# Attention scores from two float32r parts instead of three bf16 parts, with the heads of a unit split over the two halves of the array's rows

## What is computed

```python
# x: (4, 512, 256); ctx: (4, 1024, 256); 16 heads of 16
q = split_heads(layernorm(x) @ Wq.T + bq)
k = split_heads(ctx @ Wk.T + bk)
v = split_heads(ctx @ Wv.T + bv)
score = einsum('bhqd,bhkd->bhqk', q, k) / sqrt(16)
out = einsum('bhqk,bhkd->bhqd', softmax(score), v)
x = x + tanh(g_xattn) * (merge_heads(out) @ Wo.T + bo)
# then layernorm, a gate that picks 2 of 8 experts, a shared expert, all in float32
```

## Time and profile before

| | |
|---|---|
| median of 3 runs | 741.25 us (738.51 to 744.33) |
| the profiled run | 741.77 us, its span 740.0 us |
| PE busy | 647.2 us (87%) |
| DVE busy | 501.3 us (68%) |
| ACT busy | 426.1 us (58%) |
| POOL busy | 242.4 us (33%) |
| granted PE clock, mean | 0.943 of 2.4 GHz |
| chain that ended last | PE 66%, issue 14%, DVE 7%, POOL 5%, DMA 3% |

### The profile page before, as it was taken

The page is one execution under the profiler, slowest core; times in us unless marked ns, Lnnn a source line. Parts: engine busy times, 40 slices in busy tenths (PEclk is TensorE's granted clock), DMA queues, the critical chain, the costliest instruction groups (busy, mean ns, idle before and its releaser), DMA issues.

```text
span 740.0 us, 12662 instructions
## 1 busy us (share of the span) xinstructions
PE 647.2 (87%) x3616; PEld 338.5 (46%) x3616; DVE 501.3 (68%) x829; ACT 426.1 (58%) x842; POOL 242.4 (33%) x240
## 2 busy tenths in 40 slices
PE   3788677879999999999999999978886969999990
PEld 3677451223233323333333332344364758888880
DVE  5799889748888888888888888547536734433430
ACT  3665244647777777777777777745523214544440
POOL 8342224033422443134000122100175503545542
PEclk9899897979999999999999999999987989999995
DMA  8879687925696687977566340010029994665545
GB/s 276 285 223 317 194 211 169 162 47 102 108 218 181 185 175 142 202 194 166 77 100 85 60 85 1 20 39 0 9 107 356 418 277 95 96 97 94 85 46 138
DMA packets 82858, 108.11 MB, mean 146 GB/s; under 512 B 16528, under 2 KB 64570, under 8 KB 81853
## 3 DMA queue, kind: packets, MB, share of 16 engines
q1 hardware_dynamic: 72080, 78.88, 45.7%
q0 software_dynamic: 10736, 28.71, 15.0%
HBM read 62.10 MB, written 47.35 MB: 148 GB/s over the span
## 4 chain that ended last, share of the span: by engine, by line
PE 66%; issue 14%; DVE 7%; POOL 5%; DMA 3%; another core or an unknown queue 2%; SPq 1%; POOLq 1%; ACT 0%; DVEq 0%; ACTq 0%
PE psO L1464 16%; PE psS L1437 16%; PE psM L1419 13%; PE psH L1682 7%; POOL parts L581 3%; PE psY L1708 3%; PE psX L1532 2%; PE psH L1638 1%; PE psH L1679 1%; PE psX L1670 1%; PE psH L1693 1%; DMA acc<-ysb,ids 1%; PE psO L1507 1%; PE psM L1437 1%
## 5 line engine op out<-in xcount | busy, mean ns | idle before, releaser
L810 ACT ACTIVATE pr<-psS 128x512 f32<-128x512 f32 x488 | 266.6, 595 | 109.2 <-PE psS L1437 109.0
L1073 DVE TENSOR_REDUCE mneg<-psM 128x1 f32<-128x1024 f32 x240 | 282.6, 1220 | 68.6 <-PE psM L1419 68.5
L1437 PE MATMUL psS<-qst,kst 99*128 99x512 bf16 x488 | 153.8, 388 | 12.1 <-DMA qst<-msb 11.5
L1464 PE MATMUL psO<-pr,vt 128*32 128x512 f32 x1024 | 138.3, 612 | 0.0
L1419 PE MATMUL psM<-kst,qst 96*128 96x512 bf16 x480 | 127.4, 386 | 6.4 <-DVE mneg L1073 4.1
L1437 PEld LDWEIGHTS psS<-qst,kst 99*128 99x128 bf16 x488 | 39.9, 97 | 160.5 <-ACT pr L810 129.9
L720 POOL DMA_INDIRECT acc<-ysb,ids x39 | 60.2, 1543 | 74.7 <-ACT ysb L933 43.9
L1419 PEld LDWEIGHTS psM<-kst,qst 96*128 96x128 bf16 x480 | 46.3, 98 | 65.5 <-DVE mneg L1073 10.6
L567 POOL TENSOR_TENSOR msb<-mcp,none 16x128 bf16<-16x128 f32 x16 | 6.2, 389 | 209.1 <-ACT mcp L787 209.0
L1682 PE MATMUL psH<-wall,zgT 128*128 x234 | 70.3, 437 | 0.0
L1308 DVE TENSOR_TENSOR rg<-psH,rs 128x256 f32<-128x256 f32 x39 | 16.6, 424 | 68.5 <-ACT rs L921 65.1
(11 more groups left out here) (244 smaller groups left out, 869.0 us busy)
## 6 DMA issues: line engine op xcount, KB each, us to landing
kst<-k_parts SPq DMA_DIRECT2D x96, 128.0 KB, 5.8
w_parts<-wraw POOLq DMA_DIRECT2D x14, 768.0 KB, 4.7
wall<-w_parts SPq DMA_DIRECT2D x7, 1536.0 KB
v_pad<-vst SPq DMA_DIRECT2D x16, 512.0 KB, 7.6
vt<-v_pad SPq DMA_DIRECT2D x16, 512.0 KB, 7.6
wraw<-wexp POOLq DMA_DIRECT2D x9, 768.0 KB, 6.7
k_parts<-parts SPq DMA_DIRECT2D x16, 384.0 KB, 6.1
qst<-q_parts SPq DMA_DIRECT2D x96, 64.0 KB, 5.3
```

The costliest lines, as they stand in the source:

```text
L810: nc.scalar.activation(pr[:, slot, j], score_bank(s, j), ACT.Exp, scale=SCALE).then_inc(e_done, 1)
L1073: V.tensor_reduce(mneg[:, parity, i:i + 1], psM[:, i % 2], X_AXIS, ALU.max, negate=True).then_inc(m_free, 1)
L1437: mm(score_bank(s, j), kst[:, slot, j, kt * P:(kt + 1) * P], qst[:, slot, j], start=True, stop=True).then_inc(s_full, 1)
L1464: last = mm(psO[j * VW:(j + 1) * VW, u % 2], vt[:, u, k, j * VW:(j + 1) * VW], pr[:, k % 4, j], start=(k == 0), stop=(k == KT - 1), skip_g ...
```

## The change

Q and K are kept as two parts of type float32r (about float32, fewer bits in each product) for three of bf16; three products of parts are summed for six. With 16 rows each these are 48 rows, with the two parts of the maximum 50. So two heads fit above each other: heads 0 and 1 of a unit have rows 0 to 49, heads 2 and 3 rows 64 to 113 (`rows_of`), and a matmul uses one half of the array's rows.

- ACT makes part 0 in one pass; DVE makes part 1 in one operation straight from `psF`, and now it is this one that frees `psF`. `kf`, `third_parts` and `k_ok` go.
- The ones in `kst` come from a small strip in SBUF by two DMAs, not from a POOL memset of the whole rows.
- POOL splits a maximum in two operations; SP sends it in four DMAs, two for each half.
- The maximum tiles are taken in another order (`max_of`): even ones from heads 2 and 3, odd ones from 0 and 1. In a step the two halves of a maximum tile stand behind one score each, and the score is in the other half of the rows.

```diff
-TERMS = ((0, 0), (0, 1), (1, 0), (1, 1), (0, 2), (2, 0))
+TERMS = ((0, 0), (0, 1), (1, 0))
 SROWS = len(TERMS) * DH
-MROWS = SROWS + 3
+PARTS = 2
+MROWS = SROWS + PARTS
+HALF = 64
+HH = 2
...
-    q_parts = dram("q_parts", [NB, 3, D, NQ], BF16)
-    k_parts = dram("k_parts", [NB, 3, D, NK], BF16)
+    q_parts = dram("q_parts", [NB, PARTS, D, NQ], F32)
+    k_parts = dram("k_parts", [NB, PARTS, D, NK], F32)
...
-        kst = sb("kst", [MROWS, NG, HG, NK], BF16, sB)
-        qst = sb("qst", [MROWS, NG, HG, NQ], BF16, sB)
+        kst = sb("kst", [HALF + MROWS, NG, HH, NK], F32R, sB)
+        qst = sb("qst", [HALF + MROWS, NG, HH, NQ], F32R, sB)
...
+        def max_of(i):
+
+            h = HH * (1 - i % 2) + i // 2 // QT
+            return h, i // 2 % QT, h * QT + i // 2 % QT
+
+        def rows_of(h, n):
+            return slice(HALF * (h // HH), HALF * (h // HH) + n)
...
+            def load_max(n, u):
+
+                for s, ready in enumerate((m_chain, mt_split)):
+                    sp.wait_ge(ready, n + 1)
+                    for half in range(2):
+                        row = HALF * half + SROWS + s
+                        sp.dma_start(qst[row:row + 1, u].bitcast(F32),
+                                     msb[half * HH * QT:(half + 1) * HH * QT, u % 2, s, :].bitcast(F32)).then_inc(m_ld[u], 16)
...
-            nc.gpsimd.memset(kst[SROWS:MROWS], 1.0).then_inc(ones_k, 1)
-            pool.wait_ge(ones_k, 1)
+            nc.gpsimd.memset(strip[:], 1.0).then_inc(strip_ok, 1)
...
                 nc.gpsimd.tensor_tensor(msb[:, parity, 0], mcp[:], none[:].to_broadcast([HG * QT, P]), ALU.subtract).then_inc(m_chain, 1)
-                pool.wait_ge(m_chain, 3 * n + 1)
-                nc.gpsimd.tensor_tensor(mcp[:], mcp[:], msb[:, parity, 0], ALU.subtract).then_inc(m_chain, 1)
...
+                pool.wait_ge(m_chain, n + 1)
+                nc.gpsimd.tensor_tensor(msb[:, parity, 1], mcp[:], msb[:, parity, 0].bitcast(F32), ALU.subtract
                                         ).then_inc(mt_split, 1)
...
-                    act.wait_ge(k_ok, i + 1)
-
                     act.wait_ge(qk_st[c], 32 * (b + 1))
-                    bias = bq_s[:, 0 if c == 2 else 1, m:m + 1]
-                    nc.scalar.activation(kf[:, m], psF[:, m], ACT.Identity, bias=bias)
                     nc.scalar.activation(parts[:, c, m, 0], psF[:, m], ACT.Identity,
-                                         bias=bias).then_inc(f_taken, 1)
+                                         bias=bias_of(c, m)).then_inc(f_hi, 1)
...
-                    dve.wait_ge(f_taken, 2 + 6 * b + 2 * c + m + 1)
-                    chain(V.tensor_tensor(kf[:, m], kf[:, m], parts[:, c, m, 0], ALU.subtract), base + m + 1)
-                    V.tensor_copy(parts[:, c, m, 1], kf[:, m]).then_inc(r_ok, 1)
+                    dve.wait_ge(f_hi, 6 * b + 2 * c + m + 1)
+                    V.scalar_tensor_tensor(out=parts[:, c, m, 1], in0=psF[:, m], scalar=bias_of(c, m),
+                                           in1=parts[:, c, m, 0].bitcast(F32), op0=ALU.add, op1=ALU.subtract).then_inc(f_taken, 1)
...
+                rows = rows_of(j, MROWS)
+                mm(score_bank(s, j), kst[rows, slot, j % HH, kt * P:(kt + 1) * P], qst[rows, slot, j % HH], start=True,
                    stop=True).then_inc(s_full, 1)
...
                     score(0)
+                    maximum(0, 0)
                     score(1)
+                    maximum(0, 1)
                     values(b, u, k)
                     score(2)
+                    maximum(1, 0)
                     score(3)
-                    for j, off, i in tiles:
...
+                    maximum(1, 1)
```

More of the change, by code:

```diff
@@ L129, in build @@
                    ("tL", [P, 3, DT, BLK], F32R)]
-        parts, vst, kf, wA_raw, ctxt, zA, wAH, wAL, tH, tL = (sb(*a, sa) for a in a_names)
+        parts, vst, wA_raw, ctxt, zA, wAH, wAL, tH, tL = (sb(*a, sa) for a in a_names)
         sa.close()
@@ L409, in first_unit @@
                 load_unit(0, 0)
+            sp.wait_ge(strip_ok, 1)
+            for half in range(2):
+                row = HALF * half + SROWS
+                sp.dma_start(kst[row:row + PARTS].rearrange("s u h t -> s u (h t)").bitcast(F32),
+                             strip[:].unsqueeze(1).to_broadcast([PARTS, NG, HH * NK])).then_inc(ones_k, 16)
             stores(0, True)
@@ L1358, in early @@
                         pe.wait_ge(m_free, 2 + i)
[L1359 removed]
+                    h, qt, _ = max_of(i)
+                    rows = rows_of(h, SROWS)
                     for half in range(2):
                         last = mm(psE[:, half * BLK:(half + 1) * BLK],
[L1362 to L1363 removed]
+                                  qst[rows, 0, h % HH, qt * P:(qt + 1) * P],
+                                  kst[rows, 0, h % HH, half * BLK:(half + 1) * BLK], start=True, stop=True)
                     last.then_inc(m_full, 1)
@@ L1410, in _, with max_half @@
             phase_a(NB - 1, True)
-            def max_tile(t, slot, i):
-                h, qt = divmod(i, QT)
-                pe.wait_ge(m_free, t + 1)
-                for half in range(2):
-                    last = mm(psM[:, i % 2, half * BLK:(half + 1) * BLK],
-                              qst[0:SROWS, slot, h, qt * P:(qt + 1) * P],
-                              kst[0:SROWS, slot, h, half * BLK:(half + 1) * BLK], start=True, stop=True)
-                last.then_inc(m_full, 1)
+            def max_half(t, slot, i, half):
+                h, qt, _ = max_of(i)
+                rows = rows_of(h, SROWS)
+                if half == 0:
+                    pe.wait_ge(m_free, t + 1)
+                last = mm(psM[:, i % 2, half * BLK:(half + 1) * BLK],
+                          qst[rows, slot, h % HH, qt * P:(qt + 1) * P],
+                          kst[rows, slot, h % HH, half * BLK:(half + 1) * BLK], start=True, stop=True)
+                if half:
+                    last.then_inc(m_full, 1)
+            def max_tile(t, slot, i):
+                max_half(t, slot, i, 0)
+                max_half(t, slot, i, 1)
             def score_tile(s, slot, kt, j):
@@ L1481, in score, with maximum @@
                             score_tile(8 * n + k + LEAD, slot, kt, j)
+                    def maximum(a, half):
+                        for j, off, i in tiles[a:a + 1]:
+                            if off == 2 and i == 0 and half == 0:
+                                pe.wait_ge(unit_ld[(u + 2) % NG], 16 * 12 * (b + 1 + (u + 2) // NG))
+                            max_half(AHEAD + TILES * n + j, (u + off) % NG, i, half)
                     score(0)
+                    maximum(0, 0)
                     score(1)
+                    maximum(0, 1)
                     values(b, u, k)
                     score(2)
+                    maximum(1, 0)
                     score(3)
-                    for j, off, i in tiles:
-                        if off == 2 and i == 0:
-                            pe.wait_ge(unit_ld[(u + 2) % NG], 16 * 12 * (b + 1 + (u + 2) // NG))
-                        max_tile(AHEAD + TILES * n + j, (u + off) % NG, i)
+                    maximum(1, 1)
                     if k == MAX_TURN and exists(last, u + 1):
```

87 lines of the change are left out of this document (36 added, 51 removed).

## The result

| | before | after |
|---|---|---|
| median of 4 runs | 740.8 us (738.5 to 744.3) | 757.7 us (745.6 to 765.2) |
| ratio, run against run | 1 | 1.0108 (95%: 1.0061 to 1.0155) |
| profiled run, its span | 740.0 us | 763.4 us |
| PE busy | 647 us | 647 us |
| DVE, ACT, POOL busy | 501, 426, 242 us | 486, 414, 187 us |

The ratio puts the changed kernel at 749 us; run again on another chip it came to 1.0148 (1.0055 to 1.0241), 754.7 us median. So it is 1 to 1.5% slower: 742 was 7 to 10 us short, inside the range of 720 to 775. The ratios leave out the disturbed runs, those more than 1.5% above the fastest of their kernel, and the profiled run of after (765 us) is one. So a second trace of the same kernel (*after again*, span 755.2) stands beside it, whose lines of code are one further down.

The account below looks back on a forecast made before the run. The prediction took a latency loop of scores, values and exponentials (2.88 us a step) to bound the attention, and DVE the projections. 741.8 - 17 - 3 + 19 + 1.5 = 742.3, less 0.5 between run and median: 742 us, range 720 to 775.

Parts of the forecast that it names:

- The loop: Attention step: scores, values and exponentials wait on each other; two exposed float32r loads lengthen it from 2.88 to 3.09 us.
- S1 to PV: Attention step: time from the score of head 1 to the values, claimed 0.42 us and not 0.32.
- attention +19: Attention behind the stall: units 1.32 us longer, 14.4 of them, +19 us; likeliest case, chance 0.43.
- The projections, -17: Stage ahead of the attention: less DVE and POOL work and fewer PE waits, -17 us, bounds -10 and -20.
- about half goes: 6 us: Last two projection batches: of PE's 12.2 us of waits for the early maxima about half goes, 6 us.
- the 3 us at their end: End of the projections: the twelve reductions ahead of the attention start 3 us earlier, without POOL's third parts.
- The maxima's stall, -3: Unit 0 of the attention: PE's 7.6 us wait for the split maxima shortens, -3 us, bounds 0 and -7.6.
- The last 87 us, +1.5: Steps without maxima, parted by router matmuls: a few exposed loads and one more DMA, +1.5 us (0 to 3).
- Serial halves: Rival, attention: row halves run one after the other, loop 3.33 us, +52, total 775; chance 0.13 of the slower side's 0.23.
- The clock I had as a rival: Rival, attention: PE falls to 1.2 GHz, 4 us a step for part of the stage, 790 and more; chance 0.06.
- the number of mode changes stays at two a step: Attention: changes of array tiling mode, which drain the array, were claimed to stay at two a step.
- the 110 ns between the two rows: Float32r matmul behind a wait 500 ns, bf16 score 390: +0.11 us, taken to agree with a plain load of 107 ns.

Follow-up runs that it names:

- bf16 halves: Changed kernel with everything float32r in Q, K and the maxima's parts as bf16, same row halves and order: 716.3 us, ratio 0.968 to before.
- block order: Changed kernel with the maximum halves in a block behind the score of head 3 again, still in row halves: 769.1 us.
- the split: Changed kernel with a step's values in two parts of 256 queries, one moved behind the last score: 728.5 us; with the start flag corrected 723.1 us, ratio 0.976.
- warm tail: Changed kernel plus six needless full-array matmuls where PE waits in the tail: 750.5 us, ratio 1.0155 to before.
- Warm all: Changed kernel plus those six needless matmuls in the tail and three more in the projections, ahead of the sixth early maximum tile: 744.3 us, ratio 1.0035 to before.
- same-half kernels: Changed kernel and its bf16 version, each maximum half put in the same array rows as the score before it: 1047.8 us in float32r, 993.2 us in bf16.

## Why the prediction was right and where it was wrong

- **The loop.** Right, and by its mechanism. Step 3.09 predicted, 3.10 measured; unit 24.85 and 24.86; S1 to PV 0.42 and 0.44; halves within 0.05 of the scores, 0.01; attention +19, and +19.6 from 320.5 to 340.1. That last agreement is partly luck: 109 steps at a unit of 24.86 for 23.52 make 18, and the rest is half rate, which at the attention's start lasted to 158 us before, to 156 in this run and to 138 in after again, whose stage is only 14.5 longer. The bf16 halves show both loads to be the 0.21, the block order that no maximum is in the loop, and the split that the values are.
- **The projections, -17.** Wrong: -11.2 and -9.6. The first two batches won more than I gave them (8): PE's transposes of the third batch's x moved from 61.75 to 49.72, 12.0 us, since DVE came down to 12.13 a batch, where I had 12.2 (the new operation takes 747 ns for my 650, the subtractions of `tL` 683 for 1166), and left PE alone as the bound. The step that failed is "about half goes: 6 us" for the last two batches. They and the 3 us at their end, -9 together, came out 1 to 2 us longer. The waits did go: PE stands idle for 8.3 us of this stretch, for 16.4 before. But two terms that I had put at nothing took it back. One is PE's own time for the 16 early maximum tiles, whose two loads and changes of shape now show between matmuls over 128 rows. Before, and then after:

```profile
69.20 0.63 PE L1391 MATMUL psF<-tL,wAH 128*128 128x512 f32 x2
69.76 0.61 PE L1361 MATMUL psO<-kst,qst 96*128 96x512 bf16 x2
...
70.67 0.62 PE L1391 MATMUL psF<-tH,wAL 128*128 128x512 f32 x2
```
```profile
58.41 0.61 PE L1399 MATMUL psF<-tL,wAH 128*128 128x512 f32 x2
58.96 0.73 PE L1369 MATMUL psO<-kst,qst 48*128 48x512 f32 x2
...
60.19 0.62 PE L1399 MATMUL psF<-tH,wAL 128*128 128x512 f32 x2
```

The stretch around a tile takes 1.78 for 1.47 us with no wait in either: 0.3 each, 5 us for 16. The other is half rate, 14 us of it in after and 21 in after again for 8 before, so about 3 and 6 more lost; I took the clock as something that only comes back when a wait is removed. Among the waits that are left is one for the first unit's K parts, now 512 KB a store, 2.3 us and 0.5; I had called those bytes hidden.
- **The maxima's stall, -3.** The term was the wrong one. 7.6 us became 5.1, where I had near 4, and 0.6 in after again, and none of it shows in the restart. That hangs on POOL's wait for `bo`: it ended at 147.74 before and ends at 137.49 and 139.10 in the two traces of after, 10.3 and 8.6 earlier, and PE starts 5.65, 5.09 and 5.09 us behind it. How fast PE comes to the place, at half rate or not, only sets how long it stands there.
- **The last 87 us, +1.5.** Wrong, and the largest term: +17.4 and +13.0 from last reduction to last values. I had counted "a few exposed loads". There are about two pairs a step for ten steps, and with them a new change of shape to the router's matmuls: 0.49 x 10 = 5, of which one half is the loads. The rest is half rate: a tail at full clock takes 61.8 in warm tail, and the 59.6 of before less its 3 to half rate, with the 5, makes 61.
- **The sum.** 742 against 749 to 752 by the two ratios. Up to the last maximum I had -20 + 19, and it was -10.8 + 19.6 in the profiled run and -9.2 + 14.5 in after again: 6 to 10 too good. The tail was 12 to 16 short, and behind the last values the run gave 3 back. Warm all, 1.0035, shows where it comes out with less half rate in the tail. That the total is off by no more than 1 to 1.5% is partly luck: the first two batches won 12 where I had 8, and that hid a part of the 10 and more lost right behind them.
- **The rivals.** Serial halves fell by the step of 3.10 and the starts of the halves. The clock I had as a rival, with a chance of 0.06 and for the middle of the attention, where it stayed at 1.00. It made most of the miss all the same, at the edges. That a change of tiling mode drains the array, which the prediction has from the Trainium skill ("TensorEngine Tiling (Array Packing)", key properties), I had dismissed with "the number of mode changes stays at two a step". That is true of the steps with maxima and false of the tail, where 0.24 us a step agree with the rule, and of the early maximum tiles, where I didn't count. Last, I took the 110 ns between the two rows for a whole load at 107 ns; it is the difference of two loads, 183 and 92 ns.

## What to carry to other kernels

Work taken off an engine is worth nothing while a latency loop bounds it, but it makes room: look at once for what lay in the loop only because the engine was full (here, half of the values; -3% with the change, +7% without it, both against before). Count changes of matmul shape and exposed loads in every stage, the projections' and the tail's too, and not only in the one that the change is about. And before crediting PE with time, look at the granted clock around its waits, in more than one trace: here it was lower after the change in both edge stages, and took back a part of what was won.

## What the runs showed of the hardware

- **The clock stayed low over serial matmuls of 48 and 50 rows.** A step of eight such matmuls and four column tiles of values, PE recorded as 100% busy, stayed at 1.2 GHz for 590 us, in float32r and in bf16. The same matmuls two by two in both row halves rose to 2.4 GHz, if only after 17 to 55 us at the start of the attention, and those over 96 and 99 rows run at 0.99. The clock rose again in the same-half kernels only among the router's matmuls over 128 rows (at 778 and 733 us). The Trainium skill ("TensorE: Matmul & The Clock Gate", the HAM clock gate) ties the clock to how busy PE has been; by that the same-half kernels should have been fast, and the measurement decides.
- **Row halves run side by side**, loads included: 305 of 312 scores of the attention that don't wait have the maximum half within 0.01 us of their start. The Trainium skill ("TensorEngine Tiling (Array Packing)", key properties) says so of tiles in general, and the trace agrees.
- **A load of 50 x 128 takes 183 ns in float32r and 92 in bf16**, and behind a wait or behind column tiles the difference is all on the path: 500 ns for 390 of a matmul of 512 columns. Between matmuls over 128 rows it shows too, and the bf16 halves still lose 0.24 us a step of the tail there, which I put down to the change of shape.
- **The same subtraction on DVE takes 1166 ns beside POOL and 683 without it.** `tL` of 128x512, both inputs in SBUF: before, POOL makes third parts next to it; after, it has none to make. No run changes that alone.
- **The clock varies from run to run in the same code**: 0.82 or 1.00 from 60 to 98 us, 5.4 us apart.
